# Context attention on one core: scores in pairs six items ahead of the turns, maxima two items ahead of the reciprocals, exponentials ahead of the copies

## The reference

```python
q = (x @ Wq.T + bq).reshape(b, s1, h, d)              # h = 16 heads, d = 8
kv = (y @ Wkv.T + bkv).reshape(b, s2, 2, h, d)
k, v = (kv[:, :, 0], kv[:, :, 1])
q = _ln(q, qn_w, qn_b) * scale
k = _ln(k, kn_w, kn_b)
attn = jnp.einsum('bihd,bjhd->bhij', q, k)
attn = jnp.where(padding_mask[:, None, None, :], attn, -jnp.inf)
p = jax.nn.softmax(attn, axis=-1)
ctx = jnp.einsum('bhij,bjhd->bihd', p, v).reshape(b, s1, c)
out = ctx @ Wo.T + bo
```

## Time and profile before

| | us |
|---|---|
| median of 3 runs | 665.38 (664.64 to 667.9) |
| the profiled execution | 667.24 |
| its span in the profile | 665.3 |
| PE busy in the span | 555.7 (84%) |
| DVE busy | 468.7 (70%) |
| ACT busy | 309.1 (46%) |
| POOL busy | 178.3 (27%) |

### The profile page before, as it was taken

How to read it: one execution, slowest core, us unless ns; L and a number is a source line. 1 busy time by engine, 2 the same in 40 slices (tenths; PEclk the granted TensorE clock), 3 DMA queues, 4 the chain that set the end, 5 groups by cost and what they waited for, 6 DMA issues and landing times.

```text
span 665.3 us, 20734 instructions
## 1 busy us (share of the span) xinstructions
PE 555.7 (84%) x8471; PEld 425.8 (64%) x8471; DVE 468.7 (70%) x1830; ACT 309.1 (46%) x906; POOL 178.3 (27%) x217
## 2 busy tenths in 40 slices
PE   6968778679995699989999999966988898889847
PEld 4535543367884688888888888854656664656535
DVE  2978538846334677777777777761798998998882
ACT  3778636225555444344444444444545454555501
POOL 4255629236000000000000000003366347544700
PEclk9979879697997555555555555557888998998896
DMA  9900000010002000000000000000000000000000
GB/s 318 415 5 2 1 3 0 2 46 1 0 1 96 3 4 4 3 5 3 4 4 4 4 4 3 5 2 1 0 1 2 0 1 0 1 1 0 1 0 9
DMA packets 6257, 16.07 MB, mean 24 GB/s; under 512 B 2657, under 2 KB 3433, under 8 KB 5649
## 3 DMA queue, kind: packets, MB, share of 16 engines
q1 hardware_dynamic: 5744, 14.47, 6.0%
q10 hardware_dynamic: 416, 0.26, 0.1%
HBM read 14.60 MB, written 0.13 MB: 22 GB/s over the span
## 4 chain that ended last, share of the span: by engine, by line
PE 38%; DVE 30%; ACT 15%; issue 11%; POOL 5%; DMA 1%; DVEq 0%; ACTq 0%; POOLq 0%
PE bank L1713 7%; PE bank L1620 6%; PE bank L1781 6%; ACT esp L668 3%; PE bank L1571 2%; DVE ssum L1163 2%; ACT a L655 2%; ACT e L670 2%; PE bank L1558 2%; DVE w L1218 2%; DVE rz L1198 2%; DVE opre L1139 2%; POOL T L437 2%; DVE asp L1153 2%; DVE opre L1140 2%
## 5 line engine op out<-in xcount | busy, mean ns | idle before, releaser
L473 POOL MEMSET ctxT<- 128x128 f32 x1 | 0.3, 317 | 285.5 <-DVE xres L1205 285.5
L1620 PE MATMUL bank<-esp,qblk 128*128 128x1 f16 (+1 forms) x2048 | 66.8, 166 | 12.0 <-ACT esp L668 12.0
L1620 PEld LDWEIGHTS bank<-esp,qblk 128*128 128x128 f16 x2048 | 61.4, 104 | 17.2 <-ACT esp L668 17.2
L1620 PE MATMUL bank<-hsp,kT 128*128 128x2 f16 x2048 | 63.5, 166 | 2.0 <-DVE hsp L1191 1.9
L1620 PEld LDWEIGHTS bank<-hsp,kT 128*128 128x128 f16 x2048 | 59.5, 104 | 2.1 <-DVE hsp L1188 1.7
L655 ACT ACTIVATE a<-opre 128x4 f32<-128x4 f32 x64 | 13.1, 205 | 80.7 <-DVE opre L1142 80.7
L1231 DVE SCALAR_TENSOR_TENSOR T<-bank,bct,T 128x256 f32<-128x256 f32 x112 | 46.4, 472 | 2.2 <-PE bank L1794 2.2
L1218 DVE TENSOR_TENSOR_SCAN qblk<-ctxT,bank 128x512 f32<-128x512 f32 x32 | 37.7, 1207 | 5.7 <-PE bank L1781 5.3
L662 ACT ACTIVATE gact<-bank,lgate 128x16 f32<-128x16 f32 x64 | 17.7, 276 | 45.7 <-PE bank L1620 45.7
L1218 DVE TENSOR_TENSOR_SCAN w<-kT,bank 128x512 f32<-128x512 f32 x32 | 37.5, 1203 | 1.1 <-PE bank L1781 1.1
L1781 PE MATMUL bank<-maskb,T 128*128 128x512 f32 x64 | 37.4, 711 | 0.5 <-ACT T L740 0.5
(11 more groups left out here) (331 smaller groups left out, 1412.1 us busy)
## 6 DMA issues: line engine op xcount, KB each, us to landing
w<-in_w_dram SPq DMA_DIRECT2D x2, 2048.0 KB
ctxT<-in_ctxT_dram SPq DMA_DIRECT2D x8, 256.0 KB, 6.4
wqkv<-in_qkvT_dram SPq DMA_DIRECT2D x1, 1536.0 KB, 12.2
w<-in_mw_dram SPq DMA_DIRECT2D x1, 1024.0 KB, 5.0
lw<-in_lw_dram SPq DMA_DIRECT2D x1, 960.0 KB, 23.4
rows<-in_rows_dram SPq DMA_DIRECT2D x1, 772.0 KB, 9.2
wqkv<-in_fw_dram SPq DMA_DIRECT2D x1, 532.0 KB, 3.5
T<-in_mask_dram SPq DMA_DIRECT2D x1, 512.0 KB, 6.0
```

Source lines behind the costliest of these rows:

```text
L1620: return pe.matmul(out, lhsT, rhs, start=start, stop=stop, skip_group_check=True)
```

## The change

PE: `x_scores` is now called for two items at a time and waits only for the maxima of the two items that had these two banks before. Pairs of scores and pairs of turns alternate, and the scores are six items ahead of the turns (before: a whole batch ahead). The value product of a batch stands one to two turns pairs later than before, behind the pair of turns at the end of a batch. DVE: the reciprocal of an item stands two maxima behind its own maximum instead of one, the heads of a batch come three batches later instead of two, between a maximum and a reciprocal, and the copy of a batch's fourth item stands behind the first maximum and reciprocal of the batch after next. ACT: five exponentials first, then in each batch two copies, two exponentials, one copy, two exponentials. What each engine computes, the buffers, the banks and the number of instructions stay as they were.

```diff
@@ scalar
-            for i in range((B + 1) * XG):
-                if i < B * XG:
-                    x_exp(i)
-                if i >= XG and i % XG != XG - 1:
-                    x_copy_pt(i - XG)
+            for i in range(XG + 1):
+                x_exp(i)
+            for i in range(0, B * XG, XG):
+                for k in range(2):
+                    x_copy_pt(i + k)
+                for k in (5, 6):
+                    if i + k < B * XG:
+                        x_exp(i + k)
+                x_copy_pt(i + 2)
+                for k in (7, 8):
+                    if i + k < B * XG:
+                        x_exp(i + k)
@@ vector
-            for b in range(B + 2):
-                for g in range(XG):
-                    i = b * XG + g
-                    if i < B * XG:
-                        x_max(i)
-                    if 1 <= i <= B * XG:
-                        x_norm(i - 1)
-                if b == 0:
+            for i in range((B + 3) * XG):
+                if i < B * XG:
+                    x_max(i)
+                if i % XG == XG - 1 and i >= 4 * XG - 1:
+                    x_heads(i // XG - 3)
+                if 2 <= i < B * XG + 2:
+                    x_norm(i - 2)
+                if i == 3:
                     step.sync()
                     dve.tensor_scalar(wmean[:, :], wmean[:, :], 1.0 / AD, None, ALU.mult).then_inc(sem["a_wmean"], 1)
-                if 1 <= b <= B:
-                    x_copy_pt(b * XG - 1)
-                if b >= 2:
-                    x_heads(b - 2)
+                if i % XG == 0 and 2 * XG <= i <= (B + 1) * XG:
+                    x_copy_pt(i - XG - 1)
@@ tensor
-            def x_scores(b):
-
-                if b == 0:
+            def x_scores(i):
+
+                b, first = divmod(i, XG)
+                if i == 0:
                     pe.wait_ge(sem["qblk_ready"], 4)
                     pe.wait_ge(sem["v_evac"], B)
                     pe.wait_ge(sem["k_hat"], B - 1)
-                else:
-                    pe.wait_ge(sem["x_max"], XG * b)
+                elif b >= 1:
+                    pe.wait_ge(sem["x_max"], i + 2 - XG)
                 pe.wait_ge(sem["k_done"], b + 2)
-                for g in range(XG):
+                for g in range(first, first + 2):
@@
-            for b in range(B + 2):
-                if b < B:
-                    x_scores(b)
-                if b >= 2:
-                    x_pv(b - 2)
-                if 1 <= b <= B:
-                    for g in range(XG):
-                        x_transpose((b - 1) * XG + g)
+            for i in range(0, B * XG + 6, 2):
+                if i < B * XG:
+                    x_scores(i)
+                if i >= 6:
+                    x_transpose(i - 6)
+                    x_transpose(i - 5)
+                if i % XG == 0 and i >= 3 * XG:
+                    x_pv(i // XG - 3)
+            x_pv(B - 1)
```

## The result

The changed kernel takes 669.9 us (median; 669.25 to 671.81) against 666.41 for the kernel before in the same measurements (664.64 to 667.9). The ratio is 1.0053, 95% interval 1.0037 to 1.0069: slower, by 3.5 us, where I had forecast 4.2 us less. It is also outside my range, which ended at 663.8. (The top of that range was summed 0.2 short: 663.2 and the 0.8 of the late clock make 664.0. The measured time lies beyond either.)

What follows compares the result with a forecast made beforehand. A ring through PE, ScalarE and VectorE bounded the context attention's batches, then PE would. Start 1.34, even batches 0.35 and tail 2.5 summed to 4.2 us off the 665.38 median: 661.2, range 658.0 to 663.8 (8 in 10).

Steps and rivals of the forecast that it cites:

- the late clock: In the start: clock low until 42.69, T(4) at 45.66, time 662.0; added to dearer shape changes (rival's chance 0.22).
- the clock in the start: Context attention's start: full clock returns 4.66 us behind PE's restart, at 40.94.
- T(4): PE's turn of item 4 (items 0 to 31, four a batch): forecast at 44.80, 46.14 before, lead 1.34.
- a lead of 4.2 at the last heads: End of the context attention: start 1.34, even batches 0.35 and tail 2.5 make 4.2 us.
- Slower, by the clock: Rival, chance 0.06: PE without slack pays 0.5 for each microsecond at half clock; two more 10.24 us low stretches give 671.4.
- The even batch: Middle of the context attention: PE becomes the bound at 5.19 a batch against 5.26, gaining 0.07 each.
- my upper bound: PE's score products: a pair costs at most 1.07, the same as four at once; lower bound 0.86.
- The tail's length: From T(24), the turn of item 24, to the last heads: 8.6 against 11.1 before, gain 2.5.
- The start's order: Second batch's pairs of scores start at 36.28, 1.75 sooner; two pairs at half clock, 2.02 each, end at 40.32.
- my sum: Whole kernel: 4.2 us less, 661.2, own range 660.2 to 662.2, chance 0.47.
- GpSimd's subtraction: On wqkv behind the tail: 3.62 us, moves earlier, ends near 80.8, needed at 85.1.

Runs made afterwards that it cites:

- companions in four slices: Changed kernel, pairs of items 6, 8 and 10 joined by two idle products in the other two row slices: ratio 0.9954 to the kernel before.
- in the same two slices: Changed kernel, two idle products behind the pairs of items 6, 8 and 10, in the scores' own row slices: ratio 1.0129 to the kernel before.
- fours in two batches: Changed kernel with the second and third batches' scores taken four at a time, pairs from item 12 on: ratio 0.9978 to the kernel before.
- the fours without a fill: Scores four at a time, two turned items ahead and two behind, ACT's changed order, no products in PE's first wait: ratio 0.9901 to the kernel before.
- ACT's and DVE's orders alone: ACT's and DVE's new orders with PE's order of the kernel before: ratio 1.0063 to the kernel before.
- the kernel before with a full clock there: Kernel before with six plain 128-row products in PE's wait before the second batch's scores: ratio 0.9989 to the kernel before.
- the filled kernel: Changed kernel with four plain 128-row products in PE's wait before the second batch's scores: ratio 0.9925 to the kernel before, 662.0 us.

## Why the prediction was wrong

- **The step that failed is the clock in the start.** I wrote that the clock would return 4.66 us behind PE's restart, at 40.94, because it had done so once, and after 4.61 us at another place. It returned at 56.32, 20.0 us behind the restart. What I had taken for a fixed delay depends on what PE does. In the kernel before, PE did four-slice scores and turns after 38.03; in the changed one it did two-slice pairs and turns. The runs with companions in four slices (back at 43.38), in the same two slices (59.88), and with fours in two batches (45.26) settle that the slices at work make the difference. Even with fours it is no fixed delay: 5.4 us behind the restart in the fours without a fill (38.04), 6.1 with ACT's and DVE's orders alone (39.01), 8.1 with fours in two batches (37.14). T(4) came at 47.38 in place of 44.80, and T(8) 9.34 behind it in place of 5.19: 2.6 + 4.15 = 6.7 us, which turns a lead of 4.2 at the last heads into the 2.16 of lateness that was measured (the batches and the tail gave 0.4 more than forecast).
- **I had the right rival and refused it for the wrong reason.** "Slower, by the clock" had a chance of 0.06, because PE had held full clock at 81% busy "and will be busier". Busier it was, 98% in the low stretch. A busy PE alone did not bring the clock back. The price of the rival, 0.5 us for each low microsecond, was near: 15.4 us more of low clock than I had assumed is 7.7 by it, and the start lost 6.7.
- **The even batch was right**: 5.19 forecast, 5.18 measured, pair 1.07 against 1.06, two turned items 1.02, value product 1.01. The pair costs what my upper bound said, and PE became the bound with ACT and DVE waiting for it. So was the judgement that the even stretch gains next to nothing. The Trainium skill's span model ("TensorE: Matmul & The Clock Gate", "Measured speedup vs the span model") gave an estimate of 1.06 in the prediction, and the trace agrees.
- **The tail's length was right, the reason for its gain only half.** 8.6 forecast, 8.3 measured, from 11.1. I put the 2.5 of gain down to maxima and exponentials made earlier. But the 11.1 of before had the low stretch of 3.41 us in it, and the kernel before with a full clock there needs 9.6: of the 2.8 gained, 1.5 is the clock, and 1.3 the orders. That no low stretch fell into the new tail was luck, since nothing in my working says so.
- **With the clock full, the gain is there**: 0.9925 in the filled kernel, 5.0 us in place of 4.2. Its last heads are at 77.46 and not at the 79.4 I had named, since the full clock also covers the start, which I had counted partly at half clock (T(4) at 43.30 in place of 44.80).
- **The start's order was right, its price a bit high**: the pairs started at 36.28, and the two adjoining ones took 3.29 together at half clock, not 4.04. The second works in the other two slices; that it starts before the first has ended is how I read this, the row does not part them.
- **Missing from my sum**: 0.59 for the bias addition. I moved GpSimd's subtraction and asked only whether it would be done in time, not beside what it would run. Another 0.8 (2.74 at x_res, 3.5 at the end) came later in the program, where the low stretches fall otherwise; that was not taken apart.

## What to carry to other kernels

When a change splits products that ran side by side in the row slices into groups of half the size, it doubles their time (2 x 1.07 us for 1.07 here) and also takes rows of the array out of work; look at the granted clock of the stretch first, since a PE that is busy without a gap may still run at half speed. In this kernel the restart after a wait was the place where it showed, and two things helped there: four-slice work after the restart, or 128-row products in the wait. And count a low stretch of the old profile into the part in which it stands, before that part's time is compared with a new one. And an order that runs the scores ahead of the turns does not need pairs: moving two of the four turned items to the front of the scores gave 4.53 a batch where the pairs gave 5.18.

## What the hardware showed that I had not expected

- PE's busy time did not tell its clock. Four products of 32 rows in one slice filled a wait without a gap, and the clock fell; four of 128 rows in the same time held it. Behind the restart, pairs with turns did not bring it back (low for 20.5 to 27.3 us, until behind the first value product or, once, into the second), while with fours it was back after 6.8 to 10.2 us. Turns stood in all of these runs; what they or the value products count for was not tried by itself. Once full, the clock held through 34 us of pairs, turns and value products.
- DVE's TENSOR_SCALAR from SBUF to SBUF lasted until behind the end of GpSimd's 3.62 us subtraction: 0.94 and 1.42 us in place of 0.35 and 0.60, ending 0.15 and 0.35 behind it, while DVE's reduction of 128x128 (0.37, also from SBUF to SBUF) and its copy from PSUM (0.15) beside the same subtraction were as long as without it. The Trainium skill, "SBUF — State Buffer", section "SBUF: two separate sides", says that the two engines share a pair of ports that one instruction holds for its whole length; these two TENSOR_SCALAR rows agree.
